# Fused two-layer transformer kernel on one Trainium2 core: masked parts of the diagonal key blocks left out of the attention's weighted sum, and the queries of odd head pairs kept in reversed token order

## The chip, the cores and the metric

One Trainium2 chip, of which the kernel uses one core. The core has a matrix engine (TensorE, PE in the profile), three engines for elementwise work (VectorE or DVE, ScalarE or ACT, GpSimd or POOL) and a queue engine that issues transfers (SyncE or SP). Each engine runs its own instructions in their written order and waits for others by semaphores. The metric is the device time of one execution of the whole kernel, in microseconds; lower is better.

## The reference, cut to what matters

The kernel computes two layers on `x` of 4 x 512 x 256 float32. The first layer has a recurrent attention and a gated feed-forward network; neither is touched here. The second layer's attention, which the change is about, is this for each of 4 sequences of 512 tokens and 16 heads:

```python
q, c_kv = jnp.split(hidden_states @ Wqkv, [NH * D_QK], axis=-1)
k = (c_kv @ Wk_up).reshape(b, s, NKV, D_QK)
v = (c_kv @ Wv_up).reshape(b, s, NKV, D_V)
...
scores = jnp.einsum('bqhd,bkhd->bhqk', q, k) * scale
causal = jnp.tril(jnp.ones((s, s), bool))
scores = jnp.where(causal[None, None], scores, jnp.finfo(scores.dtype).min)
probs = jax.nn.softmax(scores, axis=-1)
out = jnp.einsum('bhqk,bkhd->bqhd', probs, v).reshape(b, s, NH * D_V)
return out @ Wo
```

The mask is causal: a query does not see keys that stand behind it. Keys and values come from a latent `c_kv` of 64 numbers for each token, so the kernel sums the latent rows with the probabilities and applies the value and output weights afterwards. After the attention comes a mixture of experts with a last product.

## The kernel before

**Tiling.** The attention goes by batches: one batch is one sequence and 128 of its queries. `ORDER = (1, 3, 0, 2)` gives the order of the four query tiles q of a sequence, so there are 16 batches n. A batch with query tile q has `width(n)` = 128 * (q + 1) keys. The 16 heads are 8 head pairs; a pair p of batch n is slot t = 8 * n + p, and e (0 or 1) is the head within the pair. All work of the attention is written out slot by slot, by hand, for each engine.

**A slot.** PE multiplies two heads' queries with the keys (`score`, L2102), two slots ahead of the others. DVE adds the mask, writes the scores to `probs` and takes the row maximum (`largest`, L2457). ACT takes the exponential and the row sum (`exponential`, L2357). DVE inverts the sum (`invert`, L2476), POOL multiplies (`normalize`, L2709), and DVE transposes each 32 x 32 block into `turned_of` (`turn`, L2471; the tile is called x_pairs in the profile for the query tiles 0 and 1, and wq_wo for 2 and 3).

**The weighted sum.** `weigh` (L2119) of batch n - 1 stands in slot 2 of batch n, and for the last batch in the tail. The 32 x 32 transpose leaves the 128 queries of a tile as four groups i of 32 queries, each on 32 partitions of its own. One matmul takes 32 keys (block j) of one query group i and one e: 32 rows x 64 columns of the array, and 256 moved columns (8 head pairs x 32 queries). So a key block takes 8 matmuls on 8 separate parts of the array (4 row groups i, 2 column groups e). A batch has 4 * (q + 1) key blocks; the last four are the diagonal ones, d = 0 to 3, of which query group i needs only those with d <= i. The rest is masked, so its probabilities are zero, and it is multiplied all the same.

**Around it.** The sum is accumulated in `av`, which lies over the four PSUM banks that the projections use in turn. `take_out` on ACT (L2366) copies it to `oT`; until that is done, no projection may fill a bank. Behind `weigh`, PE has the scores of two slots and then the projection of the next batch's queries. `project_q` (L2061) makes the queries of batch n + 1 from `hT`, 8 matmuls of 128 x 128 x 128 for four head pairs, for the rotated part ("rope") in slots 0 and 1 and for the latent part in slots 4 and 5. The rotated part goes on through ACT (`take_rope`, L2343), a swap by DMA, a product with the cosine on DVE (`rotate_query`, L2482), a product with the sine and a sum on POOL (`add_rope`, L2696 and L2699) and a DMA into `query`. `project_out` (L2133) applies the output weights in slots 6 and 7. In three of the four sequences, DVE also rotates the next sequence's keys (`rotate_key`, L2486 and L2487) in batches with n % 4 = 2 and 3.

## Time and profile before

| | |
|---|---|
| runs (3) | 1031.6 us median, 1030.43 to 1032.62 |
| profiled execution | span 1028.6 us, from its first to its last instruction |
| instructions | 25039 |
| TensorE busy | 970.8 us (94%) |
| VectorE busy | 702.0 us (68%) |
| ScalarE busy | 564.1 us (55%) |
| GpSimd busy | 435.5 us (42%) |
| granted TensorE clock | 0.998 of full speed |

The profile is of one execution; only its span is recorded, and the median of the runs is 3.0 us above that span. A float32 matmul stands in the trace as two MATMUL records, each with a weight load of its own (PEld), so 1280 matmuls of the weighted sum are 2560 records. "Busy" for PE is the time covered by at least one record; matmuls on separate parts of the array overlap, and a group's busy time counts such a stretch once. The order of a stage: the first layer, then the second layer's preparations, then the attention's slots, whose first score starts at 572.9 us and whose last stands at 970.9 us, then the experts with the last product.

### The profile page before, as it was taken

The page shows a single profiled execution, that of the slowest core. Times are in us where ns is not written, and L with a number is a line of the kernel's source. Part 1 is how long each engine was busy: PE and PEld are TensorE (multiplying, and loading weights), DVE is VectorE, ACT ScalarE, POOL GpSimd, SP SyncE. Part 2 cuts the span into 40 slices and gives each one's busy share as a digit, 9 for nine tenths or more (in the row PEclk, how much of TensorE's full clock was granted, in tenths as well). Part 3 has the DMA queues.
Part 4 walks back from the last instruction along what each step waited for, and adds up shares of the span by engine and source line. Part 5 has one row for each costly group of instructions (what it writes and reads, how often), then busy time and mean ns, then how long its engine had stood idle before and what let it go on. Part 6 is the DMA issues. An engine that isn't in the chain of part 4 may idle for free.

```text
span 1028.6 us, 25039 instructions
## 1 busy us (share of the span) xinstructions
PE 970.8 (94%) x9714; PEld 737.7 (72%) x9714; DVE 702.0 (68%) x2121; ACT 564.1 (55%) x1450; POOL 435.5 (42%) x391
## 2 busy tenths in 40 slices
PE   5887999999999999999999999999999999999978
PEld 3566897887887755675656769786978687868546
DVE  4889988988989942213223676866686668776864
ACT  3667778777778732212223465555556556655541
POOL 1221240340541711101002666775677567779710
PEclk9999999999999999999999999999999999999999
DMA  9250000000000002900002321322132213211202
GB/s 313 68 195 2 2 0 0 0 0 0 0 2 2 2 1 48 308 1 0 1 1 51 84 61 44 72 63 52 43 73 63 52 43 72 58 37 45 92 2 84
DMA packets 32812, 52.36 MB, mean 51 GB/s; under 512 B 7760, under 2 KB 17744, under 8 KB 31824
## 3 DMA queue, kind: packets, MB, share of 16 engines
q1 hardware_dynamic: 32720, 51.10, 18.0%
q8 instruction: 62, 1.02, 0.4%
q14 instruction: 30, 0.25, 0.1%
HBM read 21.98 MB, written 2.10 MB: 23 GB/s over the span
## 4 chain that ended last, share of the span: by engine, by line
PE 54%; DVE 4%; ACT 2%; issue 1%
PE quad L2102 12%; PE quad L2061 10%; PE quad L1705 8%; PE quad L2119 7%; PE quad L2005 6%; PE quad L2133 5%; PE quad L2197 1%; PE quad L2069 1%; PE quad L1591 1%; ACT act_probs L2366 1%; PE quad L2024 1%; DVE act_probs L2457 1%; DVE wq_wo L2471 1%; DVE x_pairs L2487 0%; ACT act_probs L2357 0%
## 5 line engine op out<-in xcount | busy, mean ns | idle before, releaser
L2709 POOL TENSOR_TENSOR act_probs<-act_probs,rden 128x512 f32<-128x512 f32 (+3 forms) x128 | 169.0, 1327 | 111.1 <-DVE rden L2476 111.1
L2357 ACT ACTIVATE act_probs<-act_probs,neg_max 128x256 f32<-128x256 f32 (+3 forms) x256 | 140.9, 553 | 83.3 <-DVE neg_max L2457 83.1
L2061 PEld LDWEIGHTS quad<-hT,ug_queries 128*128 128x128 f32 x1024 | 122.6, 192 | 14.1 <-issue 7.7
L2061 PE MATMUL quad<-hT,ug_queries 128*128 128x128 f32 x1024 | 124.7, 275 | 0.8 <-DVE act_probs L1720 0.5
L2457 DVE CUSTOM_DVE_ANT_0 act_probs<-quad,mask 128x256 f32<-128x256 f32 (+3 forms) x256 | 115.1, 485 | 0.3 <-issue 0.3
L1705 PE MATMUL quad<-hT,ug_raw_switch 128*128 128x512 f32 x256 | 113.9, 595 | 0.0
L1720 DVE SCALAR_TENSOR_TENSOR act_probs<-quad,ws_up,silu_keys 128x512 f32<-128x512 f32 x32 | 24.0, 750 | 97.1 <-ACT silu_keys L1715 97.1
L1715 ACT ACTIVATE silu_keys<-quad,ws_gate 128x512 f32<-128x512 f32 x32 | 22.0, 687 | 118.7 <-PE quad L1705 118.7
L1705 PEld LDWEIGHTS quad<-hT,ug_raw_switch 128*128 128x128 f32 x256 | 47.5, 190 | 55.1 <-issue 54.3
L2476 DVE RECIPROCAL rden<-den 128x2 f32<-128x2 f32 x128 | 20.3, 159 | 94.2 <-ACT act_probs L2357 94.0
L2102 PE MATMUL quad<-down_raw_out,ug_raw_switch 128*128 128x256 f32 (+3 forms) x256 | 79.5, 438 | 3.6 <-DVE neg_max L2457 3.6
L2102 PE MATMUL quad<-silu_keys,ug_raw_switch 128*128 128x256 f32 (+3 forms) x256 | 79.6, 439 | 2.8 <-DVE neg_max L2457 2.0
L2471 DVE STREAM_TRANSPOSE wq_wo<-act_probs 128x1024 f32<-128x1024 f32 (+1 forms) x64 | 70.8, 1106 | 0.7 <-POOL act_probs L2709 0.4
L1426 POOL TENSOR_TENSOR hidden<-gate_silu,hb 128x256 f32<-128x256 f32 x16 | 12.2, 766 | 122.9 <-ACT hb L969 94.7
L2133 PE MATMUL quad<-down_keys,act_probs 128*128 128x256 f32 x256 | 60.5, 380 | 0.8 <-ACT act_probs L2366 0.8
L2102 PEld LDWEIGHTS quad<-down_raw_out,ug_raw_switch 128*128 128x128 f32 x256 | 42.4, 190 | 24.7 <-issue 14.8
L2102 PEld LDWEIGHTS quad<-silu_keys,ug_raw_switch 128*128 128x128 f32 x256 | 42.0, 190 | 25.0 <-issue 13.7
L2005 PE MATMUL quad<-down_raw_out,act_probs 128*128 128x256 f32 x256 | 57.8, 387 | 2.0 <-PEq L1510 2.0
L2005 PEld LDWEIGHTS quad<-down_raw_out,act_probs 128*128 128x128 f32 x256 | 49.5, 195 | 10.1 <-issue 3.3
L2133 PEld LDWEIGHTS quad<-down_keys,act_probs 128*128 128x128 f32 x256 | 47.9, 190 | 12.2 <-issue 2.9
L2119 PE MATMUL quad<-wq_wo,latent_rows 32*64 32x256 f32 x1792 | 51.6, 377 | 4.7 <-DVE ug_raw_switch L2503 3.2
L2119 PEld LDWEIGHTS quad<-wq_wo,latent_rows 32*64 32x64 f32 x1792 | 45.0, 131 | 8.9 <-DVE ug_raw_switch L2503 3.4
(330 smaller groups left out, 2285.7 us busy)
## 6 DMA issues: line engine op xcount, KB each, us to landing
rope_swapped<-gate SPq DMA_DIRECT2D x120, 64.0 KB, 2.0
ug_raw_switch<-gate SPq DMA_DIRECT2D x60, 128.0 KB, 2.3
ug_raw_switch<-in_wmod SPq DMA_DIRECT2D x4, 512.0 KB, 7.4
x_pairs<-in_x SPq DMA_DIRECT2D x4, 512.0 KB, 8.0
x_rows<-x_pairs SPq DMA_DIRECT2D x8, 256.0 KB, 5.0
wq_wo<-in_wq_nopeT SPq DMA_DIRECT2D x1, 2048.0 KB, 8.5
wq_wo<-in_wo SPq DMA_DIRECT2D x1, 2048.0 KB, 13.2
ug_queries<-in_switch_w SPq DMA_DIRECT2D x1, 2048.0 KB, 7.6
```

The source lines that it names most:

```text
L1705: mm = k.nc.tensor.matmul(k.bank[2 * (m % 2) + w][:], self.w_ug[:, w, kt, P * m:P * m + P], k.hT[:, kt, 2 * i:2 * i + 2, 4 * C * u:4 * C * ...
L1715: k.nc.scalar.activation(self.silu[:, m % 2, :], k.bank[2 * (m % 2) + 1][:], ACT.Silu, scale=k.ws_gate[:, m:m + 1]).then_inc(self.silu_mad ...
L1720: k.nc.vector.scalar_tensor_tensor(self.act_t[:, m, :], k.bank[2 * (m % 2)][:], k.ws_up[:, m:m + 1], self.silu[:, m % 2, :], ALU.mult, ALU ...
L2005: mm = nc.tensor.matmul(bank[4 + q // 2][:, D * (q % 2):D * (q % 2) + D], act_t[:, m, P * q:P * q + P], w_down[:, ffn.place(m), :], start= ...
L2061: mm = nc.tensor.matmul(out[:, P * i:P * i + P], w[:, kt, HP * half + i, :], k.hT[:, kt, b, cols], start=(kt == 0), stop=(kt == KT - 1))
L2102: nc.tensor.matmul(score_bank[t % AHEAD][e][:, 0:width(n)], query[:, n % 2, e, p, :], keys[b % 2][:, p // 2, 0:width(n)], start=True, stop ...
L2119: mm = nc.tensor.matmul(av[LORA * e:LORA * e + LORA, i, :], val[rows, b % 2, j, :], src[rows, j, e, :, :], start=(j == 0), stop=(j == bloc ...
L2133: mm = nc.tensor.matmul(out[:, 0:D], oT[:, p, :], w_vo[:, p, :], start=(p == 0), stop=(p == NP - 1))
L2357: nc.scalar.activation(tile, tile, ACT.Exp, bias=neg_max[:, r, e:e + 1], scale=-1.0, accum_out=den[:, r, e:e + 1])\
L2457: nc.vector.tensor_tensor_reduce(probs[:, t % RING, e, 0:cols], score_bank[t % AHEAD][e][:, 0:cols], mask[:, L - cols:L], -QK_SCALE, 3e38, ...
L2471: nc.vector.transpose(turned_of[batches[n][1]][:, :, :, p, :].rearrange("p j e c -> p e j c"), probs[:, t % RING, :, 0:width(n)].rearrange ...
L2709: nc.gpsimd.tensor_tensor(tile, tile, rden[:, t % RING, :].unsqueeze(2).to_broadcast([P, 2, cols]), ALU.mult)\
```

## The change

Four things are done.

1. `weigh` leaves out masked work. For d = 0 all four query groups are summed for all 8 pairs, for d = 1 to 3 only for the pairs that need them.
2. So that this is spread evenly over the row groups, the queries of odd head pairs are kept in reversed token order: query group i of an odd pair holds what group 3 - i holds in an even one. Group 0 then has 8 pairs at d = 0 and the four odd pairs at d = 1, 2 and 3; group 1 has 8 pairs at d = 0 and 1 and the odd pairs at d = 2; groups 2 and 3 mirror them with the even pairs. Matmuls of four pairs move 4 x 32 columns. The loop over i is now outside that over e, in the order 0, 3, 1, 2, also in the blocks that are not diagonal.
3. The reversal is made in `project_q`, which moves `hT` backwards for odd pairs, and undone in `take_out`, which takes even and odd pairs by two instructions, the odd ones backwards.
4. Cosine, sine and mask follow: the two products of the rotation are made apart for even and odd pairs, and the mask has one more 128 x 128 tile, so that `largest` reads it as q + 1 tiles in either order.

```diff
-    k.cos, k.sin, k.mask = k.sbuf("rope_cos", [P, L]), k.sbuf("rope_sin", [P, L]), k.sbuf("mask", [P, L])
+    k.cos, k.sin, k.mask = k.sbuf("rope_cos", [P, L]), k.sbuf("rope_sin", [P, L]), k.sbuf("mask", [P, QT + 1, P])
...
+    EVERY, FORWARD, BACKWARD = slice(0, NP), slice(0, NP, 2), slice(1, NP, 2)
+    DIAGONAL = [[(i, EVERY if d <= min(i, ROWS - 1 - i) else FORWARD if d <= i else BACKWARD)
+                 for i in (0, 3, 1, 2) if d <= max(i, ROWS - 1 - i)] for d in range(ROWS)]
+    LAST_OF = [max(i, ROWS - 1 - i) for i in range(ROWS)]
...
+    def in_order(tokens, p):
+        return tokens[:, ::-1] if p % 2 else tokens
+
+    def mask_of(n, p):
+        q = batches[n][1]
+        return mask[:, q::-1, :] if p % 2 else mask[:, QT - q:QT + 1, :]
...
-                        mm = nc.tensor.matmul(out[:, P * i:P * i + P], w[:, kt, HP * half + i, :], k.hT[:, kt, b, cols],
+                        mm = nc.tensor.matmul(out[:, P * i:P * i + P], w[:, kt, HP * half + i, :], in_order(k.hT[:, kt, b, cols], i),
...
-                    for e in range(2):
-                        for i in range(ROWS):
-                            rows = slice(BLK * i, BLK * i + BLK)
-                            mm = nc.tensor.matmul(av[LORA * e:LORA * e + LORA, i, :], val[rows, b % 2, j, :], src[rows, j, e, :, :],
-                                                  start=(j == 0), stop=(j == blocks - 1))
+                    d = max(0, j - (blocks - ROWS))
+                    for i, pairs in DIAGONAL[d]:
+                        rows = slice(BLK * i, BLK * i + BLK)
+                        for e in range(2):
+                            out = av[LORA * e:LORA * e + LORA, i, :].rearrange("p (n c) -> p n c", c=BLK)
+                            mm = nc.tensor.matmul(out[:, pairs, :], val[rows, b % 2, j, :], src[rows, j, e, pairs, :],
+                                                  start=(j == 0), stop=(d == LAST_OF[i]))
...
-                for heads in [slice(0, NP)] if n < NB - 1 else [slice(0, HP), slice(HP, NP)]:
-                    nc.scalar.activation(to[:, heads], src[:, heads], ACT.Copy).then_inc(s["oT_taken"], 1)
+                for lo, hi in [(0, NP)] if n < NB - 1 else [(0, HP), (HP, NP)]:
+                    nc.scalar.activation(to[:, lo:hi:2], src[:, lo:hi:2], ACT.Copy)
+                    nc.scalar.activation(to[:, lo + 1:hi:2, ::-1, ::-1], src[:, lo + 1:hi:2], ACT.Copy).then_inc(s["oT_taken"], 1)
...
-                    nc.vector.tensor_tensor_reduce(probs[:, t % RING, e, 0:cols], score_bank[t % AHEAD][e][:, 0:cols],
-                                                   mask[:, L - cols:L], -QK_SCALE, 3e38, ALU.add, ALU.min,
+                    nc.vector.tensor_tensor_reduce(probs[:, t % RING, e, 0:cols].rearrange("p (w c) -> p w c", c=P),
+                                                   score_bank[t % AHEAD][e][:, 0:cols].rearrange("p (w c) -> p w c", c=P),
+                                                   mask_of(*divmod(t, NP)), -QK_SCALE, 3e38, ALU.add, ALU.min,
...
-                nc.vector.tensor_tensor(x, x, cos[:, cols].unsqueeze(1).to_broadcast([P, HP, P]), ALU.mult).then_inc(s["rope_turned"], 1)
+                for i in range(2):
+                    op = nc.vector.tensor_tensor(x[:, i::2], x[:, i::2], spread(in_order(cos[:, cols], i), [P, HP // 2, P], 1), ALU.mult)
+                op.then_inc(s["rope_turned"], 1)
...
-                nc.gpsimd.tensor_tensor(w, w, sin[:, cols].unsqueeze(1).to_broadcast([P, HP, P]), ALU.mult).then_inc(s["rope_swept"], 1)
-                pool.wait_ge(s["rope_swept"], 2 * n + half + 1)
+                for i in range(2):
+                    nc.gpsimd.tensor_tensor(w[:, i::2], w[:, i::2], spread(in_order(sin[:, cols], i), [P, HP // 2, P], 1), ALU.mult)\
+                        .then_inc(s["rope_swept"], 1)
+                pool.wait_ge(s["rope_swept"], 2 * (2 * n + half + 1))
```

On PE, the instructions around one weighted sum, the one of a batch with query tile 3, which stands among the scores of a batch with query tile 0. Here `order` counts a float32 matmul once, and L2102, L2061 and L2119 are the score, the query projection and the weighted sum. Before:

```order
910 L2102 MATMUL quad<-down_raw_out,ug_raw_switch 128x128 x2
911 L2119 MATMUL quad<-wq_wo,latent_rows 64x256 x128
912 L2102 MATMUL quad<-down_raw_out,ug_raw_switch 128x128 x4
913 L2061 MATMUL quad<-hT,ug_queries 128x128 x8
914 L2102 MATMUL quad<-down_raw_out,ug_raw_switch 128x128 x2
```

And after, where the same lines are L2113, L2072 and L2132:

```order
925 L2113 MATMUL quad<-down_raw_out,ug_raw_switch 128x128 x2
926 L2132 MATMUL quad<-wq_wo,latent_rows 64x256 x104
927 L2132 MATMUL quad<-wq_wo,latent_rows 64x4x32 x4
928 L2132 MATMUL quad<-wq_wo,latent_rows 64x256 x4
929 L2132 MATMUL quad<-wq_wo,latent_rows 64x4x32 x12
930 L2113 MATMUL quad<-down_raw_out,ug_raw_switch 128x128 x4
```

Of 128 matmuls with 256 columns, 108 stay, 16 become matmuls with 4 x 32 columns, and 4 are gone; the scores and the projection behind them stand where they stood.

## Rows read from the trace of the kernel before

**Rows 1.** Busy time by stage: stretch, its length, then each engine's busy us.

```profile
core 0: us, PE busy (x) PEld busy (x) DVE busy (x) ACT busy (x) POOL busy (x), PEclk, DMA share, GB/s
600.00:700.00 100.00, 98.55 (x1097) 78.57 (x1096) 72.02 (x218) 57.68 (x162) 68.95 (x54) 1.00 0.26 59
700.00:800.00 100.00, 98.56 (x1097) 78.58 (x1096) 73.45 (x221) 56.62 (x159) 70.13 (x55) 1.00 0.26 60
800.00:900.00 100.00, 98.57 (x1097) 78.52 (x1096) 71.83 (x217) 58.62 (x163) 69.42 (x54) 1.00 0.26 58
```

**Rows 2.** Who waited for whom, PE, 600 to 1000 us: total us, times, longest.

```profile
PE quad L2102 <- DVE neg_max L2457: 4.4, 5, 1.2
PE quad L2119 <- DVE ug_raw_switch L2503: 3.2, 1, 3.2
```

**Rows 3.** Chain of waits, 600 to 720 us: start us, us, what.

```profile
606.50 3.64 PE quad L2119 x128
...
628.60 7.24 PE quad L2119 x256
635.84 0.02 issue
635.86 1.03 ACT act_probs L2366
636.89 0.04 issue
636.94 2.05 PE quad L2061 x16
...
657.13 2.00 PE quad L2119 x64
659.13 0.02 issue
659.15 1.02 ACT act_probs L2366
660.18 1.20 ACT act_probs L2357 x4
...
664.21 1.18 DVE x_pairs L2486
665.39 1.68 DVE x_pairs L2487
667.07 0.47 DVE act_probs L2457
...
667.69 1.10 PE quad L2102 x4
```

**Rows 4.** Groups of instructions on PE by shape: records, busy us, mean ns.

```profile
L2061 PE MATMUL quad<-hT,ug_queries 128*128 128x128 f32 x1024 | 124.7, 275 | 0.8 <-DVE act_probs L1720 0.5
L2119 PE MATMUL quad<-wq_wo,latent_rows 32*64 32x256 f32 x1792 | 51.6, 377 | 4.7 <-DVE ug_raw_switch L2503 3.2 <-ACT gate L2343 0.8 <-issue 0.7
L2119 PE MATMUL quad<-x_pairs,latent_rows 32*64 32x256 f32 x768 | 22.8, 378 | 0.0
L2133 PE MATMUL quad<-down_keys,act_probs 128*128 128x256 f32 x256 | 60.5, 380 | 0.8 <-ACT act_probs L2366 0.8
L2142 PE MATMUL quad<-ug_queries,hT 128*32 128x256 f32 x128 | 7.3, 380 | 0.0
L2167 PE MATMUL quad<-hT,ug_raw_switch 32*32 32x128 f32 x128 | 2.6, 278 | 0.8 <-issue 0.8
L2188 PE MATMUL quad<-wq_wo,ug_raw_switch 32*32 32x128 f32 x128 | 1.9, 278 | 0.0
```

**Rows 5.** Groups by shape on ACT, DVE and POOL, 600 to 980 us.

```profile
L2343 ACT ACTIVATE gate<-quad 128x512 f32<-128x512 f32 x28 | 16.7, 595 | 21.0 <-PE quad L2061 21.0
L2366 ACT ACTIVATE act_probs<-quad 128x1024 f32<-128x1024 f32 x15 | 15.3, 1023 | 58.0 <-PE quad L2119 58.0
L2482 DVE TENSOR_TENSOR gate<-gate,rope_cos 128x512 f32<-128x512 f32 x28 | 20.2, 722 | 4.1 <-DMA rope_swapped<-gate 4.0
L2497 DVE TENSOR_TENSOR attn_gated<-quad,gate 128x256 f32<-128x256 f32 x15 | 6.2, 411 | 4.7 <-PE quad L2133 4.7
L2709 POOL TENSOR_TENSOR act_probs<-act_probs,rden 128x256 f32<-128x256 f32 x32 | 21.3, 670 | 31.4 <-DVE rden L2476 31.4
L2696 POOL TENSOR_TENSOR rope_swapped<-rope_swapped,rope_sin 128x512 f32<-128x512 f32 x28 | 38.9, 1388 | 0.7 <-DMA rope_swapped<-gate 0.6
```

**Rows 6.** Chain of waits in the tail, 940 us to the end.

```profile
985.74 1.48 PE quad L2119 x48
987.22 0.35 PE quad L2291 x2
987.59 0.20 DVE logit L2522
...
1001.06 0.44 DVE ug_raw_switch L2551
```

More of the change, by code:

```diff
@@ L2877, in rope_tables @@
     out["diagonal"] = np.tile(np.eye(BLK, dtype=np.float32), (P // BLK, 1))
-    out["mask"] = np.concatenate([np.zeros((P, L - P), np.float32), np.triu(np.full((P, P), -1e30, np.float32), 1)], axis=1)
+    diagonal = np.triu(np.full((P, P), -1e30, np.float32), 1)
+    out["mask"] = np.concatenate([diagonal[::-1], np.zeros((P, L - P), np.float32), diagonal], axis=1).reshape(P, QT + 1, P)
     return out
```

## The prediction

> **What bounds the kernel now.** The page comes first: TensorE is busy for 970.8 of 1028.6 us and no other engine passes 68%. A share over the whole run can hide a stage that waits for something else, so the second view is the busy time by stage [rows 1]. In the attention's slots PE is busy for 98.6 of each 100 us at full clock, DVE for 72 to 73, POOL for 69 to 70. So PE sets the pace there, and work taken from PE shortens the time unless something that lags behind it takes over. The third view, who waited for whom, says where that could be [rows 2]. Between 600 and 1000 us the largest wait of PE for another engine is for the row maximum of DVE, 4.4 us in five waits. The chain of waits shows one of them: at 657 us the chain leaves PE after a weighed sum, goes over the copy on ACT, the exponentials and DVE's key rotation, and comes back to PE's score at 667.69 us [rows 3]. The shortest batches, those of query tile 0, are also where PE waits for the copy itself: the sum ends at 635.84 us, ACT copies for 1.03 us, and the projection starts at 636.94 us [rows 3].
>
> **What the weighted sum costs.** Sums of 64, 128 and 256 records took 2.00, 3.64 and 7.24 us [rows 3]. They have 4, 8 and 16 key blocks, so a key block costs (7.24 - 2.00) / 12 = 0.437 us, for 8 matmuls on 8 parts of the array, 55 ns a matmul. All of them together keep PE busy for 51.6 + 22.8 = 74.4 us [rows 4].
>
> **What the change takes from it.** The three blocks d = 1 to 3 cost 3 x 0.437 = 1.31 us of each sum. Afterwards every part of the array has 640 columns in the four diagonal blocks where it had 1024: 256 for d = 0, and 384, half as many as before, for d = 1 to 3. If the parts run independently, 1.5 blocks go, 0.655 us a sum. If each d takes as long as its widest matmul, d = 1 still costs a full block (groups 1 and 2 move 256 columns in it) and d = 2 and 3 half a block each: one block goes, 0.437 us. A third reading prices the narrow matmuls directly. The nearest rows with 128 columns and separate parts are the experts', 64 matmuls in 1.9 us (30 ns each) and 64 in 2.6 us (41 ns each) [rows 4]. With them, 16 narrow and 4 wide matmuls cost 16 x 0.030 + 4 x 0.055 = 0.70 us or 16 x 0.041 + 0.22 = 0.88 us, and 0.61 or 0.43 us go. Those matmuls sit on 16 parts and have to be issued twice as fast as here, so their price is more likely too high than too low. The three readings give 0.43 to 0.66 us; I take 0.60 us. Fifteen of the sixteen sums stand between the slots of a busy PE: 15 x 0.60 = 9.0 us, with bounds of 6.5 and 9.8.
>
> The sixteenth stands in the tail in four parts, and all its diagonal blocks with d > 0 are in the last part, behind 987.22 us. There the chain has left PE for DVE's routing, from 987.59 to 1001.5 us [rows 6]. That part is hidden already, so nothing is gained. If the routing were shorter, it would be worth 0.6 us. For the same reason the copy and its extra instructions in the tail cost nothing.
>
> The Trainium skill, "TensorE: Matmul & The Clock Gate", Part 3 on packing, says that matmuls start and end strictly in program order. By that rule a narrow matmul would end no sooner than a wide one issued ahead of it, which is close to the reading in which each d lasts as long as its widest, and the sum would be 6.5 instead of 9.0 us. No row of before has two widths side by side.
>
> **What it adds.** *The copy on ACT.* One instruction of 1.023 us becomes two of half the size. The nearest row is 128 x 512 from PSUM, 0.595 us [rows 5], so 2 x 0.595 - 1.023 = 0.17 us more. Behind the copy on ACT stand exponentials; behind the wait on PE stands the projection. In the batches with query tiles 1, 2 and 3, the scores of two slots cover it: 4 matmuls of 256 columns alone are 4 x 60.5 / 128 = 1.9 us [rows 4]. With query tile 0 the cover is already used up, so 4 x 0.17 = 0.7 us are lost. Written backwards it might cost more; no row shows a backward access, and the price is between 0 and another 0.6 us each time.
>
> *The rotation on DVE.* 0.673 to 0.722 us for 128 x 512 become two of 128 x 256, for which the nearest row is 0.411 us [rows 5]: 0.1 to 0.15 us more, 32 times. DVE has 27 us in 100 to spare, so this is hidden, except in the stretches in which DVE rotates keys and PE comes to wait for it (657 to 667.69 us, and twice more). Two rotations lie in each: 3 x 2 x 0.1 = 0.6 us. Those three stretches also return part of the gain: the sum ahead of them ends sooner, but DVE's rotations of 1.18 and 1.68 us and its maxima stay. I take half of 3 x 0.60 for that, 0.8 us, between 0 (the chain does start at the sum) and 1.8.
>
> *Hidden edits.* On POOL, 1.388 us become two of 128 x 256, at 0.670 each [rows 5], so nothing. The mask is read in q + 1 pieces of 128 numbers by the same number of instructions; at nothing, with 27% of DVE's time as cover. `project_q` has the same matmuls with half of them moved backwards; at nothing, and this is the least certain price (below). The larger mask comes in one DMA long before its use.
>
> **The sum.** 9.0 - 0.7 - 0.6 - 0.8 = 6.9 us. Against the profiled execution: 1028.6 - 6.9 = 1021.7 us of span. The median of the runs is 3.0 us above that span, so 1031.6 - 6.9 = **1024.7 us**.
>
> **The rivals.** *A matmul costs its issue, not its columns.* Then 20 matmuls stay where 24 were, 4 x 0.055 = 0.22 us go for each sum, and 15 x 0.22 - 2.1 = 1.2 us remain: 1030.4 us. Against it stand 30 and 41 ns for narrow matmuls, below 55; for it, that they are far above the fourth of a full-width price that 16 parts would allow. Chance 0.08.
>
> *The gain is lost wherever slots are short.* PE runs into DVE or ACT in the batches of query tiles 0 and 2, not only in three stretches. Then the eight sums there bring nothing (one of them is the hidden last): 8 x 0.60 - 1.3 = 3.5 us, 1028.1 us. For it speaks that every PE wait in the slots lies in these batches; against it, that there are so few of them. Chance 0.10.
>
> *Moving a matrix backwards is slow (slower).* 256 of the 512 projection matmuls, at 124.7 / 512 = 0.244 us each [rows 4], read `hT` with a negative step, and all stand on the path. The point from which it decides is 6.9 / 256 = 27 ns, 11% of a matmul. At half the rate it costs 256 x 0.244 = 62 us: 1087 us. No row shows a negative step on any engine. Matmuls over strided pieces show no such cost (the routing's, pieces of 32 with gaps, 7.3 us for 64), which speaks for an engine that follows addresses one by one. Chance 0.07.
>
> *Neighbours on one row group do not overlap (slower).* With e inside i, two matmuls in a row now use the same 32 rows. If they ran one after the other, a block would take twice its time, the 136 blocks' worth that remain would cost 2 x 0.437 x 136 = 119 us where 70 are spent now, and the kernel would end at about 1031.6 + 49 + 2 = 1083 us. Against it: the routing's matmuls all use all 128 rows, on four column parts, and take 7.3 / 64 = 0.114 us, a quarter of the 60.5 / 128 = 0.473 us of a full-width one [rows 4]. The same section of the Trainium skill states that a weight load overlaps running matmuls only where the row group differs, which would make this rival true; by this rule 1083, and the trace does not agree with it where only the column part differs. Chance 0.03.
>
> **How the numbers follow.** The forecast's case has 0.68, its own range 1022.5 (0.655 us a sum and nothing returned to DVE) to 1027.8 (0.43 us a sum, 0.6 us more lost). 0.04 are left for a small loss by the longer access patterns on ACT and DVE, slower by a few us. Less than 0.2% (2 us) is about what a measurement of this kernel can't tell from no change. Faster by more: the forecast, the short slots and a little of the issue price, 0.79. Within it: most of the issue price and the edges, 0.09. Slower: 0.12. The range from 1021.5 to 1029.5 takes in the forecast and the short slots with the 1.1 us by which single runs differ, and leaves the issue price and the slow cases out.
>
> **What would show it.** PE's busy time in the weighed sum should fall from 74.4 to about 65 us, in sums of 1.4, 3.0, 4.9 and 6.6 us; at 68 the widest matmul sets each d. The projections should stay at 124.7 us: any other number is the backward read. The chain should show two copies of about 0.6 us behind the sum that precedes a query projection at query tile 0, and a PE wait of about 0.25 us. PE's waits for DVE's maxima should grow from 4.4 to about 6 us; if they grow to 9, the gain went there. What would make the forecast wrong is a price on the backward read, or narrow matmuls that cost as much as wide ones.

## The result, and the profile after

The changed kernel takes 1043.05 us (median of 4 runs, 1040.75 to 1043.89) against 1031.01 us (4 runs, 1029.27 to 1032.62) for the kernel before on the same chip. The ratio is 1.0106, with a 95% interval of 1.0084 to 1.0128. So it is slower, by about 11 us, where 6.9 us less were forecast.

The page of the changed kernel, its busy times:

```profile
span 1042.1 us, 24864 instructions
...
PE 971.2 (93%) x9586; PEld 736.7 (71%) x9586; DVE 733.0 (70%) x2153; ACT 565.4 (54%) x1467; POOL 437.5 (42%) x423
```

PE is busy for as long as before, in a span that is 13.5 us longer, though it has less to do. The stages show where it now stands still; the columns are those of [rows 1].

```profile
600.00:700.00 100.00, 94.37 (x1058) 75.36 (x1057) 80.19 (x224) 56.14 (x161) 68.77 (x62) 1.00 0.26 59
700.00:800.00 100.00, 94.26 (x1046) 74.90 (x1046) 77.54 (x213) 55.37 (x157) 67.10 (x60) 1.00 0.25 57
800.00:900.00 100.00, 94.81 (x994) 74.16 (x1000) 79.19 (x223) 56.40 (x158) 66.77 (x59) 1.00 0.25 56
```

In the attention's slots PE is idle for 5 to 6 us of each 100 where it was for 1.4, at the same full clock, and DVE is busy for 4 to 8 us more. Who waited for whom, PE, 600 to 1015 us, names the place:

```profile
PE quad L2113 <- DVE neg_max L2471: 18.1, 22, 1.8
PE quad L2132 <- DVE ug_raw_switch L2520: 3.5, 1, 3.5
...
PE quad L2146 <- ACT act_probs L2380: 0.8, 1, 0.8
...
PE quad L2072 <- ACT act_probs L2380: 0.7, 4, 0.2
```

The first of them was 4.4 us in 5 waits [rows 2]. The score's matmuls wait for a bank that DVE's maximum (`largest`) must free. What DVE did ahead of that maximum is in the chain of waits, 607 to 620 us:

```profile
607.35 3.10 PE quad L2132 x112
610.45 0.02 issue
610.47 0.60 ACT act_probs L2379
611.07 0.49 ACT act_probs L2380
611.56 1.41 ACT act_probs L2370 x4
...
613.07 2.44 DVE gate L2498 x2
615.51 0.60 DVE act_probs L2471
...
616.17 1.98 PE quad L2113 x4
```

L2498 is the cosine product of `rotate_query`, now two instructions. The two products alone take 2.44 us, where one of twice the size took 0.722 us [rows 5]. The groups by shape of the changed kernel, whole run, the copies from 600 to 990 us:

```profile
L2498 DVE TENSOR_TENSOR gate<-gate,rope_cos 128x256 f32<-128x256 f32 x60 | 57.4, 997 | 3.7 <-DMA rope_swapped<-gate 3.4
...
L2714 POOL TENSOR_TENSOR rope_swapped<-rope_swapped,rope_sin 128x256 f32<-128x256 f32 x64 | 50.7, 812 | 1.7 <-DMA rope_swapped<-wq_wo 0.9 <-DMA rope_swapped<-gate 0.7
...
L2072 PE MATMUL quad<-hT,ug_queries 128*128 128x128 f32 x1024 | 124.7, 275 | 1.2 <-ACT act_probs L2380 0.7 <-DVE act_probs L1720 0.5
...
L2379 ACT ACTIVATE act_probs<-quad 128x512 f32<-128x512 f32 x15 | 8.9, 596 | 49.2 <-PE quad L2132 49.2
...
L2380 ACT ACTIVATE act_probs<-quad 128x512 f32<-128x512 f32 x15 | 8.9, 591 | 0.0
```

The mean of a half-size product is 0.997 us. But the spread of its durations (shortest, median, longest in ns) shows that this isn't a price of the shape:

```profile
L2498 DVE TENSOR_TENSOR gate<-gate,rope_cos x60: 403/836/2118, 582.5 to 956.2; 128x256 f32<-128x256 f32 x60
```

The timeline of DVE and of POOL around one pair:

```profile
607.70 0.17 DVE L2491 RECIPROCAL rden<-den 128x2 f32<-128x2 f32 x1
607.78 2.44 DVE L2498 TENSOR_TENSOR gate<-gate,rope_cos 128x256 f32<-128x256 f32 x2
610.14 0.68 DVE L2471 CUSTOM_DVE_ANT_0 act_probs<-quad,mask 128x512 f32<-128x512 f32 x1
...
607.94 1.99 POOL L2728 TENSOR_TENSOR act_probs<-act_probs,rden 128x1024 f32<-128x1024 f32 x1 [0.79 <-DVE rden L2491]
```

The reciprocals (L2491, `invert`) release POOL's normalisation of the probabilities (L2728). The first product starts 0.16 us ahead of it and takes 0.40 us. The second starts while POOL works and ends 0.29 us after POOL does: POOL ends at 607.94 + 1.99 = 609.93, the pair at 607.78 + 2.44 = 610.22. It is so nearly all along: in 29 of the 30 pairs the second product waits and ends 0.28 us after a POOL instruction does; in 25 of them that is the normalisation. The same place in the kernel before:

```profile
606.93 0.67 DVE L2482 TENSOR_TENSOR gate<-gate,rope_cos 128x512 f32<-128x512 f32 x1
607.52 0.68 DVE L2457 CUSTOM_DVE_ANT_0 act_probs<-quad,mask 128x512 f32<-128x512 f32 x1
...
607.09 2.26 POOL L2709 TENSOR_TENSOR act_probs<-act_probs,rden 128x1024 f32<-128x1024 f32 x1 [0.79 <-DVE rden L2476]
```

There the one product ran for its 0.67 us, and POOL's instruction took 2.26 us instead of 1.99. POOL paid, and here nobody waits for it. In the changed kernel DVE pays, which PE waits for.

### The profile page after: what moved, and what is told of

Read it like the earlier page. It is cut to its first block, busy times and chain, and to the rows that moved or that the text cites. A ratio compares the mean times of both kernels' runs of the same rounds, so it can differ in the third digit from the quotient of the medians.

```text
span 1042.1 us, 24864 instructions
## 1 busy us (share of the span) xinstructions
PE 971.2 (93%) x9586; PEld 736.7 (71%) x9586; DVE 733.0 (70%) x2153; ACT 565.4 (54%) x1467; POOL 437.5 (42%) x423
## 4 chain that ended last, share of the span: by engine, by line
PE 43%; DVE 11%; ACT 5%; issue 1%; DMA 0%; SPq 0%; DVEq 0%
PE quad L1705 8%; PE quad L2113 7%; PE quad L2072 6%; PE quad L2132 6%; PE quad L2016 5%; PE quad L2146 4%; DVE gate L2498 3%; DVE act_probs L2471 2%; ACT act_probs L2370 2%; DVE wq_wo L2486 2%; PE quad L2210 1%; DVE x_pairs L2504 1%; PE quad L2080 1%; PE quad L1591 1%; PE quad L2035 1%
## 5 line engine op out<-in xcount | busy, mean ns | idle before, releaser
L2728 POOL TENSOR_TENSOR act_probs<-act_probs,rden 128x512 f32<-128x512 f32 (+3 forms) x128 | 166.8, 1305 | 117.1 <-DVE rden L2491 117.1
L2072 PEld LDWEIGHTS quad<-hT,ug_queries 128*128 128x128 f32 x1024 | 122.6, 192 | 14.4 <-issue 7.7
L2072 PE MATMUL quad<-hT,ug_queries 128*128 128x128 f32 x1024 | 124.7, 275 | 1.2 <-ACT act_probs L2380 0.7
L2113 PE MATMUL quad<-silu_keys,ug_raw_switch 128*128 128x256 f32 (+3 forms) x256 | 80.9, 443 | 10.2 <-DVE neg_max L2471 10.1
L2113 PE MATMUL quad<-down_raw_out,ug_raw_switch 128*128 128x256 f32 (+3 forms) x256 | 80.5, 441 | 10.2 <-DVE neg_max L2471 10.2
L2491 DVE RECIPROCAL rden<-den 128x2 f32<-128x2 f32 x128 | 20.4, 159 | 75.9 <-ACT act_probs L2370 75.7
L2471 DVE CUSTOM_DVE_ANT_0 act_probs<-quad,mask 128x128 f32<-128x128 f32 (+3 forms) x160 | 65.2, 444 | 0.0
L2113 PEld LDWEIGHTS quad<-silu_keys,ug_raw_switch 128*128 128x128 f32 x256 | 41.8, 190 | 32.9 <-DVE neg_max L2471 16.0
L2113 PEld LDWEIGHTS quad<-down_raw_out,ug_raw_switch 128*128 128x128 f32 x256 | 42.2, 190 | 31.4 <-issue 14.2
L2498 DVE TENSOR_TENSOR gate<-gate,rope_cos 128x256 f32<-128x256 f32 x60 | 57.4, 997 | 3.7 <-DMA rope_swapped<-gate 3.4
L2132 PE MATMUL quad<-wq_wo,latent_rows 32*64 32x256 f32 (+1 forms) x1728 | 48.7, 373 | 5.0 <-DVE ug_raw_switch L2520 3.5
## 6 DMA issues: line engine op xcount, KB each, us to landing
ug_raw_switch<-gate SPq DMA_DIRECT2D x60, 128.0 KB, 2.3
```

Source lines behind the costliest of these rows:

```text
L2072: mm = nc.tensor.matmul(out[:, P * i:P * i + P], w[:, kt, HP * half + i, :], in_order(k.hT[:, kt, b, cols], i), start=(kt == 0), stop=(kt ...
L2113: nc.tensor.matmul(score_bank[t % AHEAD][e][:, 0:width(n)], query[:, n % 2, e, p, :], keys[b % 2][:, p // 2, 0:width(n)], start=True, stop ...
L2132: mm = nc.tensor.matmul(out[:, pairs, :], val[rows, b % 2, j, :], src[rows, j, e, pairs, :], start=(j == 0), stop=(d == LAST_OF[i]))
L2471: nc.vector.tensor_tensor_reduce(probs[:, t % RING, e, 0:cols].rearrange("p (w c) -> p w c", c=P), score_bank[t % AHEAD][e][:, 0:cols].rea ...
L2498: op = nc.vector.tensor_tensor(x[:, i::2], x[:, i::2], spread(in_order(cos[:, cols], i), [P, HP // 2, P], 1), ALU.mult)
L2728: nc.gpsimd.tensor_tensor(tile, tile, rden[:, t % RING, :].unsqueeze(2).to_broadcast([P, 2, cols]), ALU.mult)\
```

## The experiments

Three theories were held against each other. The first: the split of the cosine product lets POOL's instruction in between, and DVE waits for all of it (POOL between the products). The second: reading a table backwards is slow on DVE. The third: the fixed cost of one more DVE instruction, or some other edit (copy, mask, projection, matmul order), costs the time. A time that follows is the median of a kernel's runs (4 to 12 of them), and the ratio that to the kernel before on the same chip, with its 95% interval. Where PE's waits for the maxima are given, they are those from 600 to 1015 us.

**One product again.** The change whole, but the cosine product is one instruction for even and odd pairs, with a table that holds the cosine in both orders. Room for it is made by moving three small buffers to the first stage's scope. The edits of table and buffers are left out here and below.

```diff
-                for i in range(2):
-                    op = nc.vector.tensor_tensor(x[:, i::2], x[:, i::2], spread(in_order(cos[:, cols], i), [P, HP // 2, P], 1), ALU.mult)
-                op.then_inc(s["rope_turned"], 1)
+                x = rope_x[n][:, half].rearrange("p (m o c) -> p m o c", o=2, c=P)
+                nc.vector.tensor_tensor(x, x, spread(cos[:, :, cols], [P, HP // 2, 2, P], 1), ALU.mult).then_inc(s["rope_turned"], 1)
```

> The changed kernel, with the cosine product of the rotation again as one DVE instruction of 128x512 for each half: the cosine table is kept in both token orders, so one access pattern serves even and odd pairs. POOL's sine product stays in two instructions, the weighted sum, the reversed queries, the two copies and the mask stay as changed. Theory A (between DVE's two half products POOL starts its normalisation on the row sums just inverted, and the second half product stands until that is over): the rotation goes back to about 0.67 to 0.72 us, PE's waits for the row maxima fall from 18.1 to about 6 us, the 0.64 us of each of the 15 sums stay gained, and the time is 1031.0 - 15 x 0.64 + 4 x 0.17 + 1, about 1023 us (1021 to 1026). Theory B (the cosine read backwards is slow on DVE): the same, since the table is read forwards here too. Theory C (the loss sits elsewhere, in the two copies on ACT, POOL's two products or the mask in pieces): 1038 to 1043 us. The clock: TensorE dropped to half of it at 989.45 us for 6.8 us in the changed kernel's profile, after 3.5 us without a matmul; before, with 3.2 us, it did not. If that follows the length of the gap, it should be gone or stay by chance, and is worth some 2 us.

Measured: 1026.75 us, ratio 0.9956 (0.9940 to 0.9971). PE's waits for the maxima:

```profile
PE quad L2115 <- DVE neg_max L2473: 5.9, 7, 1.3
```

The waits are as theory A had them, the time a little above its 1021 to 1026 us. The change without the split is faster than before, by 0.3 to 0.6%: taken together, everything else that it edits is a gain.

**Forward tables.** As above, but with two half products, each reading its own table forwards.

```diff
-                    op = nc.vector.tensor_tensor(x[:, i::2], x[:, i::2], spread(in_order(cos[:, cols], i), [P, HP // 2, P], 1), ALU.mult)
+                    op = nc.vector.tensor_tensor(x[:, i::2], x[:, i::2], spread(cos[:, i, cols], [P, HP // 2, P], 1), ALU.mult)
```

> The changed kernel with its two DVE half products, but both read the cosine forwards, from a table that is kept in both orders; nothing else differs. It tells theory A from theory B. A (POOL gets in between): no change, the second half product still takes 0.83 to 2.12 us according to the batch, and the time stays at 1041 to 1044 us. B (backward reads are slow): both half products take about 0.40 us and the time falls to 1022 to 1026 us.

Measured: 1042.82 us, ratio 1.0106 (1.0078 to 1.0134), waits of 18.1 us in 22 as in the changed kernel, and the products' durations are the same as those of the backward ones to the nanosecond or two:

```profile
L2500 DVE TENSOR_TENSOR gate<-gate,rope_cos x60: 402/836/2118, 583.6 to 957.7; 128x256 f32<-128x256 f32 x60
```

The direction of the table costs nothing on DVE; the second theory falls.

**Only the split.** The kernel before, with nothing but its cosine product made in two.

```diff
-                nc.vector.tensor_tensor(x, x, cos[:, cols].unsqueeze(1).to_broadcast([P, HP, P]), ALU.mult).then_inc(s["rope_turned"], 1)
+                for i in range(2):
+                    op = nc.vector.tensor_tensor(x[:, i::2], x[:, i::2], spread(cos[:, cols], [P, HP // 2, P], 1), ALU.mult)
+                op.then_inc(s["rope_turned"], 1)
```

> The kernel before with one edit: the cosine product on DVE in two instructions, for even and for odd pairs, both forwards. No reversal, no skipped work, one product on POOL, one copy on ACT. A (POOL gets in between): the second half product takes 0.8 to 2.1 us as in the changed kernel. DVE then has some 35 us more, and PE waits for it in the same stretches, so the loss is that of the changed kernel without its gain: PE has 0.64 us more to do in each batch, which hides part of it. 1039 to 1050 us. B (backward reads): 1031 to 1033 us.

Measured: 1044.28 us, ratio 1.0132 (1.0104 to 1.0159), 14.0 us of waits for the maxima in 22. This one edit, in a kernel that has none of the others, costs as much as the whole change did (1.0106, 1.0084 to 1.0128), as far as the intervals can tell.

**The same two products, issued first.** The changed kernel, with `rotate_query` ahead of `invert` in DVE's slot, so that the products are issued before the reciprocals release POOL.

```diff
-                if t < SLOTS:
-                    invert(t)
                 for _, n, half in due(t, 3, "rope"):
                     rotate_query(n, half)
+                if t < SLOTS:
+                    invert(t)
```

> The changed kernel with one line of DVE's slot moved: the two half products (still two, one of them backwards) stand ahead of the inversion of the row sums, on which POOL's normalisation waits. A: POOL is not released when the half products run, so both take about 0.40 us, unless POOL is still at the normalisation of the slot before. POOL's normalisation starts some 0.65 us later in these slots. The time falls to 1022 to 1028 us. B (backward reads): the second stays slow at any place, 1041 to 1044 us.

Measured: 1027.82 us, ratio 0.9965 (0.9949 to 0.9981), waits of 5.7 us in 6. DVE's and POOL's timeline at the same place:

```profile
605.07 0.72 DVE L2498 TENSOR_TENSOR gate<-gate,rope_cos 128x256 f32<-128x256 f32 x2
605.71 0.15 DVE L2491 RECIPROCAL rden<-den 128x2 f32<-128x2 f32 x1
...
605.94 1.90 POOL L2728 TENSOR_TENSOR act_probs<-act_probs,rden 128x1024 f32<-128x1024 f32 x1 [1.27 <-DVE rden L2491]
```

This pair takes 0.72 us instead of 2.44. Two instructions for one is therefore no cost worth naming, and the third theory falls too: what costs is that POOL works when the second is issued. Not every pair is as free as this one. The spread of all:

```profile
L2498 DVE TENSOR_TENSOR gate<-gate,rope_cos x60: 382/423/1523, 579.6 to 937.1; 128x256 f32<-128x256 f32 x60
```

The median fell from 836 to 423 ns, but the mean of a pair is 1.22 us (1.99 in the changed kernel), since about half of them still wait for a POOL instruction, mostly the sine product or the addition of a rotation. That is enough for the time: it can't be told from the one-product kernel's (0.9965 against 0.9956).

**Four products.** The changed kernel, with one product for each of the four heads' pairs, 128 x 128 each.

```diff
-                for i in range(2):
-                    op = nc.vector.tensor_tensor(x[:, i::2], x[:, i::2], spread(in_order(cos[:, cols], i), [P, HP // 2, P], 1), ALU.mult)
+                for i in range(HP):
+                    op = nc.vector.tensor_tensor(x[:, i:i + 1], x[:, i:i + 1], spread(in_order(cos[:, cols], i), [P, 1, P], 1), ALU.mult)
```

> The changed kernel with the cosine product on DVE in four instructions of 128x128 instead of two of 128x256. Theory A (one of them stands until POOL's normalisation is over, the others run free): one of the four takes 0.6 to 2.0 us, the other three 0.2 to 0.3 us each, and the time is that of the changed kernel within 3 us, 1042 to 1046 us. Rival (each instruction over reversed or interleaved pieces has a large price of its own): twice the loss of two, above 1052 us.

Measured: 1059.44 us, ratio 1.0250 (1.0223 to 1.0277), 28.5 us of waits for the maxima in 22. That is more than the 1042 to 1046 us expected, which counted one wait for POOL in a rotation, whatever the number of products. By the time alone it is the rival that came true, a large price of each instruction (above 1052 us); the durations decide between them. The timeline:

```profile
609.57 3.67 DVE L2498 TENSOR_TENSOR gate<-gate,rope_cos 128x128 f32<-128x128 f32 x4
613.17 0.68 DVE L2471 CUSTOM_DVE_ANT_0 act_probs<-quad,mask 128x512 f32<-128x512 f32 x1
...
609.73 1.89 POOL L2728 TENSOR_TENSOR act_probs<-act_probs,rden 128x1024 f32<-128x1024 f32 x1 [0.90 <-DVE rden L2491]
611.58 1.51 POOL L2714 TENSOR_TENSOR rope_swapped<-rope_swapped,rope_sin 128x256 f32<-128x256 f32 x2
```

The spread of the products' durations, whole run:

```profile
L2498 DVE TENSOR_TENSOR gate<-gate,rope_cos x120: 259/806/2016, 580.7 to 974.9; 128x128 f32<-128x128 f32 x120
```

The first product takes 0.27 us, and every product that waits for no POOL instruction takes 0.26 to 0.29, so the instruction has no large price of its own. The second waits for L2728 (2.02 us), the third and fourth, of 0.81 us each, for one of POOL's two sine products each (1.51 / 2 = 0.76 us a piece). DVE and POOL take turns, an instruction each; in 22 of the 30 rotations the third and the fourth both end 0.15 us after a POOL instruction. A part of the added time is of another kind: the granted clock is 0.98 in each 100 us from 600 to 900 us, where the changed kernel has 1.00.

**Only the skipping.** The kernel before, with the masked matmuls of the weighted sum left out and nothing reversed. It leaves out only products whose probabilities are zero.

```diff
-                    for e in range(2):
-                        for i in range(ROWS):
+                    d = max(0, j - (blocks - ROWS))
+                    for i in range(d, ROWS):
+                        for e in range(2):
...
-                                                  start=(j == 0), stop=(j == blocks - 1))
+                                                  start=(j == 0), stop=(j == blocks - ROWS + i))
```

> The kernel before with only the skipping: query group i leaves out the blocks d > i for all pairs, no reversed order. 48 of the 128 diagonal matmuls of 4 blocks are gone per four sums' worth (12 of 32 in each sum), but group 3 keeps all its 16 blocks. If the parts of the array run independently and the longest row group sets the end, a sum takes as long as before (7.10 us for 256 records before) and the time stays at 1030 to 1033 us. If matmuls cost by their number, 12 x 0.055 x 15 = 10 us go, 1021 us, and the reversal was not needed.

Measured: 1030.46 us, ratio 0.9993 (0.9976 to 1.0011). The sums in the chain, with 12 matmuls (24 records) fewer each, are as long as before, where they took 3.64 and 7.24 us [rows 3]:

```profile
603.47 3.64 PE quad L2120 x104
...
625.58 7.17 PE quad L2120 x232
```

From a sum's first matmul to the next line's it is 1.91, 3.64, 5.37 and 7.10 us for the four lengths in both kernels, but for one or two longer ones in each. Row group 3 has its full work in every block, and the sum is as long as that. It is the even spread that the reversal makes which shortens it, not the count of matmuls. This kernel also has the loop over e inside that over i, as the changed one; so that order of the matmuls costs and saves nothing.

**A filled wait in the tail.** The one-product kernel, with two matmuls of 128 x 128 by 512 whose results are not used, ahead of the tail's first sum. The profile of the changed kernel showed half clock there, that of before had not, and this was to price it.

```diff
+            for last in banks.before_sum(NB - 1):
+                clear(last)
+            for _ in range(2):
+                nc.tensor.matmul(bank[0][:], k.ones[:], k.hT[:, 0, 0, :], start=True, stop=True)
             pe.wait_ge(part_made, 2 * (B - 2) + 1)
```

> The kernel of e1 with two matmuls of 128x128x512 more in the tail, on ones and into a bank that the weighted sum overwrites, in the wait of PE ahead of the last batch's weighted sum (3.5 us without a matmul in e1). Their results are not used. In e1 the clock was at half for 3.4 us from 973.5 us and for 6.8 us from 990.6 us, with about 2.4 us lost between the start of that sum and the end. Theory A2 (the clock falls because of the long wait, which the change moved from 3.2 to 3.5 us): the clock stays at full speed at the first place, perhaps at both, and the time falls by 1 to 2.5 us against e1, to about 0.994 of before. Rival (the clock falls there by chance or for what went before): no change, 0.996.

Measured: 1026.48 us, ratio 0.9941 (0.9922 to 0.9959), against 0.9956 (0.9940 to 0.9971) without. The two can't be told apart, and the gain that was expected of the filled wait isn't shown. In the profiled execution the first tail sum took 1.55 us where it had taken 2.87, but another fall of the clock came at 992.3 us.

**All rotations first.** The kernel above, with `rotate_query` and `rotate_key` both ahead of `invert` and `take_value`.

```diff
-                if t < SLOTS:
-                    invert(t)
                 for _, n, half in due(t, 3, "rope"):
                     rotate_query(n, half)
-                for _, b, half in due(t, 2, "value"):
-                    take_value(b, half)
                 for b, f in key_at(t, 3, 7):
                     rotate_key(b, f)
+                if t < SLOTS:
+                    invert(t)
+                for _, b, half in due(t, 2, "value"):
+                    take_value(b, half)
```

> The kernel of e5 with the rotations of queries and keys on DVE ahead of the inversion of the row sums. It asks whether what is left of PE's waits for the row maxima (5.9 us in e1) comes from the key rotation, whose second product takes 1.6 us where POOL runs beside it. If POOL holds it up, both key products fall to 0.7 us, PE's waits fall below 4 us and the time falls by another 1 to 3 us, to about 0.992 of before. If DVE's own work makes the waits, the time stays at that of e5.

Measured: 1022.49 us (1020.44 to 1023.80), ratio 0.9899 (0.9878 to 0.9920), 4.2 us of waits for the maxima in 7. It is faster than the filled kernel, by 0.0042 in the ratio, give or take 0.0028, and faster than before. Its sine product of the keys:

```profile
L2508 DVE TENSOR_TENSOR x_pairs<-x_pairs,rope_sin 128x512 f32<-128x512 f32 x6 | 5.7, 946 | 0.0
```

The same line took 1587 ns in the filled kernel. So POOL did hold it up, and where it did not start beside POOL it now takes 0.68 us; but three of the six still meet POOL (1.21 us), and the waits are 4.2 us, not below the 4 expected. In the kernel before the second product of the key rotation had waited for POOL all along. The six in the attention, and two ahead of it with no POOL instruction beside them:

```profile
L2487 DVE TENSOR_TENSOR x_pairs<-x_pairs,rope_sin x6: 1754/1856/1956, 652.4 to 872.6; 128x512 f32<-128x512 f32 x6
L2487 DVE TENSOR_TENSOR wq_wo<-wq_wo,rope_sin x2: 684/684/684, 556.3 to 558.9; 128x512 f32<-128x512 f32 x2
```

**The same edits on the kernel before.** The filled wait and the order, without the change.

> The kernel before with the two edits of e5 and e6 alone: rotations of queries and keys on DVE ahead of the inversion, and two more matmuls in the wait of the tail. The weighted sum, the order of the queries and the cosine product (one instruction) are those of before. It tells how much of e6's 1.0% is the weighted sum's. If DVE's products beside POOL cost the kernel before something too, its waits for the row maxima (4.4 us) fall by 1 to 2 us, and it ends at 0.998 of before or a little under, 1029 to 1031 us; then some 7 to 8 us of e6 are from the sum. If most of e6's gain were from the order of DVE's instructions, this would end below 1026 us.

Measured: 1029.85 us, ratio 0.9979 (0.9965 to 0.9994), waits of 3.1 us in 3, as expected. Of the 1.0% that the all-first kernel gains, the order and the filled wait alone give 0.2%. The difference of the two ratios is 0.0080, give or take 0.0026, so some 8 us are what the rest of the change brings: the shorter weighted sums, less what the copies and the other additions cost.

**The kernel before once more.** Unchanged, one profile, to see whether its tail always runs at full clock.

> The kernel before, unchanged, for a second profile. Every kernel profiled since, also one that only splits the cosine product, shows TensorE's clock at half for 3.4 to 6.8 us from about 82 us (in the first layer, which no edit touches) and again in the tail from 972 to 993 us; the first profile of before shows neither. If the drop at 82 us comes by chance, this profile may show it. In the tail, if it follows the length of the wait (3.2 us before, 3.5 us in the others), the clock stays full; a drop here with a wait of 3.2 us would say that the tail's drop is no effect of the change.

Measured: 1033.29 us in one run, span 1031.5. A stretch of its tail:

```profile
980.00:990.00 10.00, 10.00 (x204) 5.53 (x196) 1.60 (x7) 0.81 (x2) 0.00 (x0) 0.72 0.01 2
```

and two of the tail's sums in its chain of waits:

```profile
979.63 2.87 PE quad L2119 x48
...
983.12 2.69 PE quad L2119 x48
```

The stretch of the changed kernel that answers to the first:

```profile
990.00:1000.00 10.00, 9.11 (x178) 5.03 (x178) 2.42 (x6) 0.81 (x2) 0.00 (x0) 0.69 0.01 2
```

A mean granted clock of 0.72 and 0.69 means that both spent part of these 10 us at 1.2 GHz and the rest at 2.4. The fall comes with a stretch in which PE waits for DVE (3.2 us before, 3.5 us after). It isn't an effect of the change: the kernel before has it in one execution and not in another. The fall in the first layer comes by chance too: this profile has a mean granted clock of 0.83 from 78 to 88 us, the first one of before 1.00, and the filled kernel's, unlike what the expectation says of all, is at full clock there. Against this profile the changed kernel's tail begins 990.89 - 979.63 = 11.3 us later and its span is 10.6 us longer, so the whole loss lies ahead of the tail. (One execution against one; the medians differ by 12.0 us, the ratio says 11.)

## Why the prediction was wrong

**What bounds the kernel** was right, as was the place at which a loss would come in: PE waits for the maxima of DVE. They grew to 18.1 us, not to 6.

**The weighted sum** was right. The all-first kernel and the changed one have sums of 3.01 to 3.10 and 6.63 us in the chain where 3.64 and 7.24 stood [rows 3]. The timelines, from a sum's start to the next line, give 0.63 to 0.65 us for each of the four lengths. 0.60 was taken, and 0.655 was the reading in which the parts of the array run independently. The fifteen sums of the two profiles add up to 67.1 and 57.5 us, 9.6 us instead of 9.0. The total of the records, forecast at 65 us, is of no use as a test: it is 77.3 us, since records of matmuls that overlap in a new way, and those at half clock in the tail, are longer while the sums are shorter. The prediction set 0.437 us a sum beside the rule that matmuls start and end strictly in program order, from the Trainium skill, "TensorE: Matmul & The Clock Gate", Part 3. That doesn't follow from it: groups 0 and 3, the ones with narrow matmuls at d = 1, are issued first in each block, so each of their matmuls at d = 2 may end together with the wide ones of d = 1 without holding up anything, and the rule allows the 0.655 us as well. The 0.63 to 0.65 us measured rule out the reading by the widest matmul, not the rule.

**The copy on ACT** was right in size: 0.596 + 0.591 - 1.023 = 0.16 us. The chain has 0.60 + 0.49 of it on the path, so that less than 0.1 us is lost where it shows, and PE's wait behind it, four times, rose from 0.3 to 0.7 us in all, where 0.7 us more were forecast. Its backward half costs no more than the forward one.

**The projection** was right: 124.7 us for 1024 records before and after, half of them now backwards. That rival, and with it the largest feared loss, is out. **The neighbours on one row group** don't run one after the other either: the kernel with only the skipping has them, and its sums are as long as before. The same Part 3 of the Trainium skill says that a weight load overlaps running matmuls only where the row group differs. The trace doesn't agree where only the column part differs: a sum with such neighbours throughout takes the 3.64 us that it took without them.

**The issue price** is out as well: leaving out 12 matmuls without the reversal gave nothing that can be told from no change, while the balanced sum saves what its columns say.

**The hidden edits.** The mask in pieces costs nothing: a maximum takes 484 ns on the mean, 485 before. POOL's sine products take 2 x 0.812 = 1.62 us where 2 x 0.670 was forecast and 1.388 [rows 5] measured before: 35 of the 64 take 0.72 to 0.74 us, the other 29, held up by DVE, 0.90 to 0.97. They are not quite without effect: three of the 30 second cosine products wait for one.

**The step that failed is the rotation on DVE**: "0.673 to 0.722 us for 128 x 512 become two of 128 x 256, for which the nearest row is 0.411 us [rows 5]: 0.1 to 0.15 us more, 32 times." The pair takes 2 x 0.997 = 1.99 us, so 1.27 us more, about ten times the estimate. 24 of the 30 first products take 0.40 to 0.43 us, so the second carries nearly all of it: it lasts until POOL's instruction is over, a normalisation of 0.64, 1.09, 1.57 or 1.92 us by the batch's width. The other half of the step, "this is hidden", failed with it: PE's waits for the maxima grew by 13.7 us. The row taken for the price (L2497) had the right shape and the wrong operands: one of its inputs is `quad` in PSUM, while `gate` and `rope_cos` both lie in SBUF. It wasn't that POOL was idle beside it. In 14 of its 16 places POOL's normalisation runs, and it takes 0.40 to 0.43 us all the same, as here:

```profile
699.84 0.40 DVE L2497 TENSOR_TENSOR attn_gated<-quad,gate 128x256 f32<-128x256 f32 x1
...
699.38 1.89 POOL L2709 TENSOR_TENSOR act_probs<-act_probs,rden 128x1024 f32<-128x1024 f32 x1 [4.65 <-DVE rden L2476]
```

The Trainium skill, "SBUF — State Buffer", section "Who interferes with whom", states this case: a DVE instruction with two SBUF inputs contends with a GpSimd instruction that reads SBUF, through a port pair that whoever issues first holds for a whole instruction while the other is fully blocked. By that rule the second product can't end before POOL does, and ends a fixed time after it. The trace agrees: 1.99 us of POOL, a product of 2.12 us, and 0.28 us after POOL's end in 29 of 30 pairs.

The profile of before held the warning. Two products of the same shape follow each other in the key rotation, and the second was 0.5 us longer than the first [rows 3]. Both were in fact held up by POOL, as such a product takes 0.67 to 0.69 us where POOL doesn't hold it up. The prediction used both durations and did not ask why they differ. It also gave DVE's 27 idle us in 100 as the cover. That cover is real only where DVE is not late: the maxima of a slot stand behind the product in the queue, and PE's score two slots further on can't start without them.

**Where the time went.** The stretch from the first sum to the first one of the tail, before and after:

```profile
606.43:980.47 374.04, 364.39 (x4094) 287.29 (x4093) 274.17 (x827) 209.73 (x587) 268.75 (x212) 1.00 0.25 58
607.27:990.89 383.62, 359.57 (x3973) 282.52 (x3972) 304.79 (x855) 210.61 (x602) 270.51 (x240) 1.00 0.24 57
```

It is 9.6 us longer. PE's idle time in it rose from 9.7 to 24.1 us, 14.4 us, of which 13.6 are waits for the maxima; its busy time fell by 4.8 us. The 15 sums alone fell by 9.6 us. The other 4.8 us are in the scores and the projections: counted from each matmul's start to the next one's, less the idle time, they went from 127.6 to 130.0 and from 97.3 to 99.6 us. The kernel with only the split has the same (129.8 and 99.6), the one-product kernel hardly any (128.0 and 97.6, with the same backward reads), so this belongs to the waits as well. Against the second profile of before, this stretch is 9.9 us longer (373.75 us there), what lies ahead of it 1.4 us longer and the tail 0.7 us shorter, which makes the 10.6. So the gain was made and is in the result; the waits for DVE took it and as much again. This is the rival "the gain is lost wherever slots are short" in kind, but not in size: it let 3.4 of the 6.9 us be lost, the waits grew by 13.7, and it wasn't among the cases that end slower.

Two slips of the prediction's sums matter little: half of 3 x 0.60 is 0.9, not 0.8, and of the eight sums that stand in the batches of query tiles 0 and 2 none is the hidden last one, so that rival leaves 7 x 0.60 - 1.3 = 2.9 us. Without the failed step the forecast would have been near, but high: the one-product kernel gains 0.0044 of 1032 us, 4.5 us, between 3.0 and 6.2, where 6.9 were forecast.

## What to carry to other kernels

Before a DVE instruction with two inputs in SBUF is split, or moved behind something that releases POOL, look at what POOL runs beside it: the second part may last until that POOL instruction is over, whatever its own size. Price an added instruction by a row that has its operands in the same memories and the same neighbours, and take two unequal durations of one shape as a question. Skipping masked blocks on a row-packed array paid here only where it lightened the fullest row group. And where such a product must be split, issuing it ahead of the instruction that releases POOL can bring the loss back: here the ratio went from 1.0106 to 0.9965.

## What the runs showed of the hardware

The exclusion between DVE and POOL alternates by instruction: with four products instead of two, the third and fourth each waited for a further POOL instruction (0.81 us for a product that takes 0.26 to 0.29 alone), and the kernel went from 1043 to 1059 us. It did not touch a DVE product of the same 128 x 256 with one input in PSUM: 0.40 to 0.43 us beside the same POOL instruction. Reading or writing an operand backwards cost nothing on three engines: PE's moving operand (124.7 us either way), ACT's output (596 and 591 ns) and DVE's table (403/836/2118 and 402/836/2118 ns). And the granted clock in the tail fell to half in one execution of the kernel before and not in another, after the same wait of 3.2 us, with 2.9 us between their spans (1028.6 and 1031.5 us): a difference of that size between two single profiles says nothing about an edit.
